# VectorE's loop in two attention stages: unrolled over one batch item instead of two

## The reference, cut to what matters

```
h = layernorm(x) * (1 + ca) + sa
x = x + ga * attn(h)

layer 0: 16 heads of 64, causal softmax, then Wo and a bias
layer 1: 8 heads of 128;
         scores = (Q + embed_bias) K^T + relative_shift((Q + pos_bias) rel_k^T)
         a = softmax(scores), out = (a V) w_out + b_out
```

## Time and profile before

| | us |
|---|---|
| median of 3 runs | 2787.06 (2785.5 to 2788.62) |
| the profiled execution, device time | 2791.02 |
| span of the profiled execution, first to last instruction | 2789.3 |
| outside its span | 1.7 |

### The profile page before, as it was taken

How to read it: one execution, slowest core, us unless ns; L and a number is a source line. 1 busy time by engine, 2 the same in 40 slices (tenths; PEclk the granted TensorE clock), 3 DMA queues, 4 the chain that set the end, 5 groups by cost and what they waited for, 6 DMA issues and landing times. The chain is left out here.

```text
span 2789.3 us, 61608 instructions
## 1 busy us (share of the span) xinstructions
PE 2515.3 (90%) x19690; PEld 2068.7 (74%) x19752; DVE 1871.5 (67%) x5884; ACT 1424.9 (51%) x3993; POOL 656.9 (24%) x1179
## 2 busy tenths in 40 slices
PE   4999999997999899999997999958997886999888
PEld 3888888886888698999996888846665474666566
DVE  4777777775677477878876666656775225777587
ACT  3888888885444355555554323214545132545444
POOL 0000000000111000000000101146774025777322
PEclk9999999998999899999998999979998897999899
DMA  5000000002000354555554000046553744655100
GB/s 148 2 2 1 0 0 1 1 1 64 1 1 1 120 157 151 160 161 160 159 160 99 1 1 0 1 147 173 156 149 80 89 48 116 162 153 147 36 14 18
DMA packets 196188, 212.33 MB, mean 76 GB/s; under 512 B 12628, under 2 KB 179940, under 8 KB 194676
## 3 DMA queue, kind: packets, MB, share of 16 engines
q1 hardware_dynamic: 195956, 209.64, 28.3%
HBM read 108.95 MB, written 90.65 MB: 72 GB/s over the span
## 5 line engine op out<-in xcount | busy, mean ns | idle before, releaser
L709 DVE TENSOR_REDUCE a_nmax<-bank 128x2 f32<-128x512 f32 x256 | 165.0, 686 | 155.9 <-PE bank L637 155.9
L1180 ACT ACTIVATE a_p<-a_p,a_nmax 128x256 f32<-128x256 f32 x256 | 128.3, 502 | 227.3 <-DVE a_nmax L1368 227.3
L221 POOL TENSOR_TENSOR delta<-y,arena 128x256 f32<-128x256 f32 x32 | 24.7, 771 | 814.9 <-ACT y L214 814.9
L1823 ACT ACTIVATE a_p<-bank 128x1024 f32<-128x1024 f32 (+1 forms) x256 | 193.5, 808 | 25.2 <-PE bank L1878 21.4
L1450 ACT ACTIVATE f_silu<-bank 128x512 f32<-128x512 f32 x128 | 76.7, 599 | 211.6 <-PE bank L125 210.7
L1766 POOL TENSOR_SCALAR_AFFINE_SELECT a_p<-a_p 128x512 f32<-128x512 f32 x256 | 163.0, 637 | 0.0
L2032 DVE TENSOR_REDUCE a_nmax<-bank 128x4 f32<-128x1024 f32 x128 | 155.6, 1216 | 2.8 <-PE bank L1865 2.8
L902 ACT ACTIVATE f_hidden<-bank,arena 128x512 f32<-128x512 f32 x128 | 87.8, 686 | 126.7 <-PE bank L125 126.7
L1019 DVE SCALAR_TENSOR_TENSOR f_acc<-bank,f_cw,f_acc 128x128 f32<-128x128 f32 x448 | 125.5, 344 | 37.8 <-PE bank L965 37.0
L965 PEld LDWEIGHTS bank<-arena,f_hidden 128*128 128x128 f32 x1024 | 133.8, 191 | 19.3 <-DVE f_acc L1019 3.6
L965 PE MATMUL bank<-arena,f_hidden 128*128 128x128 f32 x1024 | 142.7, 278 | 3.7 <-DVE f_acc L1019 3.0
(11 more groups left out here) (328 smaller groups left out, 7736.8 us busy)
## 6 DMA issues: line engine op xcount, KB each, us to landing
pos_dram<-a_pos SPq DMA_DIRECT2D x128, 383.0 KB, 2.8
a_stack<-rows_dram SPq DMA_DIRECT2D x128, 320.0 KB, 4.1
rows_dram<-a_cut SPq DMA_DIRECT2D x192, 192.0 KB, 2.4
a_shifted<-pos_dram SPq DMA_DIRECT2D x128, 256.0 KB, 2.7
f_merged<-f_staged SPq DMA_DIRECT2D x16, 578.0 KB, 9.0
gate<-gates_dram SPq DMA_DIRECT2D x32, 256.0 KB, 11.4
arena<-in_task SPq DMA_DIRECT2D x4, 1156.0 KB, 8.5
x<-in_x SPq DMA_DIRECT2D x4, 512.0 KB, 8.3
```

What stands on the lines that cost most here:

```text
L709: dve.tensor_reduce(nmax[:, at.ring(2), h, :], s_ps[h][:].rearrange("p (t k) -> p t k", t=NT), AX_X, ALU.max, negate=True).then_inc(s["nma ...
L1180: i = act.activation(p[:, at.ring(4), t, :], p[:, at.ring(4), t, :], ACT.Exp, bias=nmax[:, r, t:t + 1], accum_out=sums[:, r, t:t + 1])
L1823: act.activation(p[:, b4.ring(2), first:end], sT_ps[:, first:end], ACT.Exp).then_inc(s["exp"], 1)
```

## The change

DVE's `walk` in both attentions gets `unroll` = 1 instead of 2. The `step` functions, their waits and their work are the same, and so are the walks of PE, ACT, POOL and SP, which stay at `unroll` = 2.

```diff
@@ -732,7 +732,7 @@   (attention0, block.vector)
                     if at.p == 3 and at.shift(-4).real:
                         row_stats(dve, n, at.shift(-4), s["added"])
 
-                walk(dve, PER, 2, LEAD, LAG, step)
+                walk(dve, PER, 1, LEAD, LAG, step)
```

## The result

The changed kernel takes 2771.75 us (median of 4 runs, 2769.63 to 2774.86), the kernel before on the same chip 2787.84 (4 runs, 2785.5 to 2791.47): a ratio of 0.9941, 95% interval 0.9929 to 0.9954, or 16.1 us less. The forecast was 2778.0 with a range down to 2772.0. The direction was right and the size was not: 16 us instead of 9. The profiled execution took 2774.86 us (span 2773.2) against 2791.02 of the one before, 16.2 us less.

What follows compares the result with a forecast made beforehand. PE was taken to set the pace in both attentions, DVE mattering only where PE waits for it. -10.0 us in attention1 and +0.9 in ffn1 sum to -9.1: from 2787.06 to 2778.0 us, range 2772 to 2784.5.

Steps and rivals of the forecast that it cites:

- The cause of the dear back edges: DVE's loops: code comes in pieces of 128 instructions, three stay; a lap touching four refetches its head, 3.9 us in attention1.
- The five dear back edges go: attention1, DVE: the shorter lap ends five fetch stalls, 2.0 us of PE time each, -10.0 us; bounds 3.7 and 13.3.
- PE's own wait: attention1, PE's L1252 waiting for DVE's L1347: 8.6 us in five times, bounding a stall's cost at 1.7 us each.
- The last lap, 63.04: attention1's lap ending without a dear back edge, against 65.7 us for the others: bounds a stall's cost at 2.7 us.
- The straight pair, 64.97: attention1, pair at 1004 to 1069 without back edges at either end: bounds a stall's cost at 0.7 us.
- Thirteen cheap back edges each in `attention1` and `attention0`: DVE's short-lap branches, 0.3 us each, hidden under other work: cost 0; without cover 5 us and 3 us.
- Items 1 and 14 as laps: Both attentions, DVE: two items per stage move from straight code into the loop with register operations added: cost 0.
- `ffn1` moved into a fourth piece: ffn1, DVE: shifted code makes its single back edge cost 2.4 to 2.8 us; +0.9 us in time, bounds 0 and 2.0.
- B: attention1: gain mostly eaten as position-score transfers bind instead, 0.7 us per back edge, 2784.3 us; chance 0.22.
- D: attention1: slower, each taken branch refetches even in a short lap, 13 stalls instead of 5, 2804 us; chance 0.05.
- C: attention1: everything DVE lost comes back, small waits behind each stall too, 2772 us; chance 0.11.
- A: Whole kernel, the forecast itself: gain between 5.6 and 13 us, likeliest 9, time 2774 to 2781.4; chance 0.62.

Runs made afterwards that it cites:

- run 2: Kernel before with only attention0's DVE loop unrolled over one item, attention1 keeping its lap of two: 2770.8 us, ratio 0.9953.
- run 3: Kernel before, no loop changed, with 120 one-element memsets ahead of DVE's first wait in the load phase: 2767.71 us, ratio 0.9939.
- run 5: Changed kernel with 48 one-element memsets ahead of DVE's first wait: 2771.07 us, ratio 0.9939.
- run 6: Kernel before with 120 memsets ahead, plus one unread DVE reduction at the end of each attention1 lap: 2771.82 us, ratio 0.9936.
- run 7: Kernel before with 120 memsets ahead, plus two unread DVE reductions at the end of each attention1 lap: 2781.64 us, ratio 0.9974.
- run 8: Kernel before with 120 memsets ahead, plus three unread DVE reductions at the end of each attention1 lap: 2791.48 us, ratio 1.0015.
- run 10: Kernel before with 100 memsets ahead, plus two large and three small unread DVE reductions per attention1 lap: 2791.26 us, ratio 1.0006.
- run 4: Kernel before, no loop changed, with 10 one-element memsets ahead of DVE's first wait: 2791.01 us, ratio 1.0018.

## Why the prediction was right in direction and wrong in size

**What bounds the kernel**: right. PE sets the pace, and all of the gain is PE time in `attention1` that waited for DVE.

**The cause of the dear back edges**: right, and now shown by runs, not only read from packets. Three loops (`attention1` in runs 2 and 3, `ffn1` in the changed kernel and in run 5) went from one price to the other by moving alone. By the Trainium skill ("Runtime: NRT & Kernel Launch", section "Instruction fetch mechanics") a taken branch stalls for a fetch where its target is outside the two blocks that are held. The trace agrees that the target must still be held, but the packets of DVE's code have 8.2 KB, and a lap that touches three such pieces pays no stall.

Pieces of twice the size (256 instructions), of which two stay, would not explain it. `ffn0`'s back edge takes 2.7 to 3.3 us in the profiles of all twelve kernels. Its code stands at six different places in them: moved by 0, 10, 100, 120, -331 and -283 instructions. A lap of 379 instructions overruns two such pieces only from 122 of the 256 places that its head can have (130 if one counts 387), and no choice of place for the kernel before puts all six among them.

**"The five dear back edges go", 2.0 us each**: this step failed, by size. The kernel gained 3.65 us per lap, 18.3 for the five, and 20.3 for the stage with its first and last items. That is more than the 16.9 us of DVE's idle time, which I had said can't be exceeded: DVE was late at other places too. My three bounds were all too low, each for a reason of its own:

- *PE's own wait, 1.7 each.* I counted one line's idle time. In the earlier trace rows PE stands idle for 262.80 - 252.32 = 10.5 us in four laps, 2.6 each, since other lines wait too. And PE's busy time there is itself 4.2 us longer than the 248.10 that the same work takes after the change. Some 1.7 of it is one stretch at the lower clock (last section); for the rest the matmuls took longer, and why isn't shown. Less the 0.1 us that PE still idles after the change, 10.4 + 4.2 = 14.6 us, or 3.65 per lap. The idle time stood in my own rows.
- *The last lap, 63.04, as the measure of a lap without a stall.* The same steps take 61.97 in the changed kernel. The last lap has no taken branch, but it wasn't free of the trouble: its two steps at the item boundary (1397.07 to 1405.83) take 8.76 us instead of 7.60, and a packet of queue 14 falls into 1399.0 to 1400.5. That this fetch is the cause is likely and not shown. Measured against this lap, a stall looked 1 us cheaper than it was.
- *The straight pair, 64.97.* The start of the stage is slow by itself: the same steps take 64.45 in the changed kernel, where a steady pair takes 62.05. It was no reference at all.

Runs 6 to 8 show what the 2.0 would have been right for: a single delay of 3.0 us. A fetching lap is late at four places, and in run 10 three small delays beside the large one cost another 0.8 us (up to 0.2 of it clock), since the large one had used up PE's reserve of 1.0 us already.

**Thirteen cheap back edges each in `attention1` and `attention0`, 0**: right. The branch takes 0.22 to 0.28 us under the cover of the work ahead of it; `attention0` has not changed.

**Items 1 and 14 as laps, 0**: nothing in the traces speaks against it; it wasn't measured by itself.

**`ffn1` moved into a fourth piece, +0.9**: the stall came as forecast, 2.75 us in a range of 2.4 to 2.8. DVE's L1531 behind it, and the PE line that waits for it (answers to the earlier trace rows):

```profile
1658.71 0.69 DVE L1531 TENSOR_TENSOR f_hidden<-f_silu,bank 128x512 f32<-128x512 f32 x1 [2.34 <-issue]
...
1659.45 1.16 PE L1504 MATMUL bank<-arena,f_hidden 128*128 128x128 f32 x8 [0.66 <-DVE f_hidden L1531]
```

PE waits 0.66 us there; the stage grew by 0.9 us in the mean of twelve executions. The term holds, within a scatter of its own size. So with the gain put right the sum would have been -18.3 + 0.9 = -17.4 us, and 16.1 were measured.

**The rivals.** *B* (the transfers take the gain) is out: waits for `a_shifted` ahead of L74 grew from 8.0 to 12.9 us between 1100 and 1433, and PE doesn't notice. *D* (each taken branch refetches) is out: 13 back edges at 0.2 us. *C* (all that DVE lost comes back) was nearest, at 2772; its reason was right as well, that small waits behind each stall go too. (A and C together have chances of 0.73, so the 0.75 that I gave to "faster" was slightly more than they hold.)

## What to carry to other kernels

Where a loop's back edge takes 3 us on an engine and 0.3 in the next stage, compare the lap's place with the instruction packets before changing the loop: here 120 instructions without use in the load phase gave the same 0.6% as the edit, and every edit ahead of a loop can give or take it. When costing a stall of a feeder, measure the starved engine's whole loss over equal work (idle time and longer busy time), and be wary of a lap without a stall that is taken from the ends of a stage. Here a delay cost next to nothing up to the reserve and everything beyond it, and small ones beside a large one weren't small.

## What the runs showed of the hardware beyond that

**Reaching further into a fourth piece saved nothing.** One long stall, or two shorter ones (run 4) of 3.7 us together. From the branch's end to the head of the lap, a lap with a fourth piece paid 3.9 to 4.4 us in the kernel before, 2.7 to 3.8 and a second stall behind it in run 4, 2.7 to 3.1 in `ffn1` and 2.7 to 3.3 in `ffn0`. What sets the price within these bounds isn't known.

**A stall can cost TensorE's clock too.** Windows of the kernel before, around the back edge at 1231 us (the eighth column is the granted clock):

```profile
1235.00:1238.60 3.60, 1.86 (x15) 1.49 (x14) 2.04 (x11) 0.00 (x0) 0.00 (x0) 1.00 0.30 79
1238.60:1242.01 3.41, 3.19 (x13) 2.90 (x12) 3.34 (x15) 1.94 (x6) 0.00 (x0) 0.50 0.32 118
1242.01:1245.00 2.99, 2.99 (x26) 2.99 (x26) 2.28 (x6) 2.33 (x7) 1.21 (x2) 1.00 0.62 186
```

After 3.6 us in which PE was busy for half the time, its clock stands at the lower level (1.2 GHz) for 3.4 us, and it executes 13 matmuls where the next 3 us have 26. In the profiled execution of the kernel before this happened at one of the five back edges, in run 4's at four of them:

```profile
1239.50:1242.90 3.40, 3.40 (x13) 3.40 (x14) 3.33 (x15) 2.04 (x6) 0.00 (x0) 0.50 0.31 115
```

In the eight steady items of the changed kernel and of runs 3, 6 and 7 it never does. It isn't a matter of fetches: it also happens behind the delays of runs 8 and 10, in laps without one packet. Its cost is small here. Run 4's pairs took 66.3 us; from the last L1371 of one lap to the last of the next, the four laps with such a stretch took 65.87 to 66.99 us, and the one without 66.14. In the kernel before the lap with it took 65.32, the others 65.24 to 66.23.
